# A two-stage gated layer on one core: first-stage tiles only centred, their roots applied a step later in silu and gate

## The reference

```
def _layernorm(x, axis=-1, eps=1e-05):
    m = jnp.mean(x, axis=axis, keepdims=True)
    v = jnp.var(x, axis=axis, keepdims=True)
    return (x - m) / jnp.sqrt(v + eps)
...
        for e in range(E):                      # E = 4, each 512 x 512, Wg = Wu = Wd = ctx[e]
            g = jax.nn.silu(jnp.einsum('bsd,fd->bsf', hidden_states, Wg[e]))
            u = jnp.einsum('bsd,fd->bsf', hidden_states, Wu[e])
            y = jnp.einsum('bsf,df->bsd', g * u, Wd[e])
            out = jnp.where((expert_ids == e)[..., None], y, out)
...
    x = x + jnp.tanh(g_xattn[0]) * _L0_xattn_ref(_layernorm(x, axis=-1), itok_BxS_13_99985, ctx_2048, ctx_2048, ctx_2048)
    x = x + jnp.tanh(g_ffn[0]) * _L0_ffn_ref(_layernorm(x, axis=-1), ...)   # shared MLP + top 2 of 16 experts
```

## Time and profile before

| | |
|---|---|
| median of 3 runs | 477.52 us (477.21 to 477.65) |
| the profiled execution's own time | 477.07 us |
| its span, first to last instruction | 474.9 us |
| granted TensorE clock, mean | 0.997 |
| PE busy | 459.0 us (97% of the span) |
| DVE, ACT, POOL busy | 329.8, 254.8, 209.0 us |

### The profile page before, as it was taken

One profiled execution on the slowest core, in us unless ns is written; L12 is line 12 of the kernel. 1 busy time (PEld: TensorE's weight loads), 2 busy tenths in 40 slices (PEclk: granted clock), 3 DMA queues, 4 the chain that ended last, 5 costly groups with the idle time before them and its releaser, 6 DMA issues.

```text
span 474.9 us, 7818 instructions
## 1 busy us (share of the span) xinstructions
PE 459.0 (97%) x2493; PEld 392.5 (83%) x2493; DVE 329.8 (69%) x726; ACT 254.8 (54%) x379; POOL 209.0 (44%) x176
## 2 busy tenths in 40 slices
PE   2899999999999999999999999999999999999995
PEld 1477878888888888888888999999999999999994
DVE  6689999998986844488649776766666666676442
ACT  5664445545553443542436566566556766656441
POOL 0513444555442475435177343434425444342543
PEclk9999999999999999999999999999999999999998
DMA  8643666886664542363379988898868988888364
GB/s 302 196 167 126 195 198 210 277 258 236 214 212 162 179 122 112 85 82 46 44 192 203 286 287 265 274 285 262 254 206 251 270 256 268 258 277 243 47 129 91
DMA packets 30476, 95.28 MB, mean 201 GB/s; under 512 B 4976, under 2 KB 7024, under 8 KB 29936
## 3 DMA queue, kind: packets, MB, share of 16 engines
q0 software_dynamic: 17056, 43.92, 37.7%
q1 hardware_dynamic: 13104, 50.98, 31.3%
q10 hardware_dynamic: 288, 0.01, 0.0%
HBM read 67.77 MB, written 28.70 MB: 203 GB/s over the span
## 4 chain that ended last, share of the span: by engine, by line
PE 92%; DVE 4%; DMA 1%; issue 1%; ACT 0%; POOL 0%; POOLq 0%; DVEq 0%
PE psG L1370 50%; PE psY L1370 30%; PE psT L1375 8%; PE psG L1626 1%; DMA front<-in_x,idx 1%; DMA tok_i<-in_ids 1%; PE psY L1387 1%; PE psG L1399 1%; DVE stats L991 0%; PE psY L1506 0%; POOL out L560 0%; PE psY L1670 0%; DVE xh_sb L964 0%; DVE gu L980 0%; PE psY L1532 0%
## 5 line engine op out<-in xcount | busy, mean ns | idle before, releaser
L1370 PE MATMUL psY<-arena 128*128 (+1 forms) x366 | 89.2, 394 | 0.0
L1370 PEld LDWEIGHTS psY<-arena 128*128 128x128 f32 x366 | 67.7, 188 | 13.9
L519 POOL DMA_INDIRECT ht<-out,idx x32 | 32.6, 1018 | 68.3 <-PE psT L1375 52.5
L1370 PE MATMUL psY<-slot,arena 128*128 128x512 f32 x240 | 59.0, 394 | 0.0
L1114 DVE TENSOR_TENSOR slot<-raw,slot 128x1536 fp32r<-128x1536 f32 x25 | 43.8, 1757 | 21.0 <-ACT slot L660 21.0
L1370 PE MATMUL psG<-arena 128*128 x228 | 57.0, 399 | 0.0
L1114 DVE TENSOR_TENSOR arena<-raw,arena 128x1536 fp32r<-128x1536 f32 x24 | 42.0, 1757 | 17.5 <-ACT arena L660 17.4
L1370 PEld LDWEIGHTS psY<-slot,arena 128*128 128x128 f32 x240 | 44.3, 188 | 9.2 <-ACT xh_sb L704 0.2
L1370 PE MATMUL psG<-arena,slot 128*128 128x512 f32 x216 | 51.3, 392 | 0.0
L1370 PEld LDWEIGHTS psG<-arena 128*128 128x128 f32 x228 | 41.5, 188 | 8.5 <-issue 0.4
L1370 PEld LDWEIGHTS psG<-arena,slot 128*128 128x128 f32 x216 | 40.1, 188 | 8.2
(11 more groups left out here) (246 smaller groups left out, 811.3 us busy)
## 6 DMA issues: line engine op xcount, KB each, us to landing
raw<-in_w SPq DMA_DIRECT2D x48, 768.0 KB, 5.5
padded<-xh_sb SPq DMA_DIRECT2D x19, 256.0 KB, 2.2
raw<-in_w SPq DMA_DIRECT2D x12, 192.0 KB, 4.3
raw<-in_ctx_t SPq DMA_DIRECT2D x2, 1024.0 KB, 8.1
ht<-in_ctx_t SPq DMA_DIRECT2D x1, 1024.0 KB, 11.1
xh_sb<-in_ctx_t SPq DMA_DIRECT2D x1, 1024.0 KB, 9.1
out<-log_sb SPq DMA_DIRECT2D x4, 256.0 KB, 7.9
ht<-out,idx POOLq DMA_INDIRECT x33, 4.2
```

The costliest lines, as they stand in the source:

```text
L519: pool.indirect_dma_start(ht[:, n, :], None, halves_of_out, slots(e * NA + a, 0)).then_inc(g_here[n], 16)
L1370: ins = pe.matmul(ps, left[a], right[b], start=n == 0 and m == 0, stop=n == total - 1 and m == 2)
```

## The change

It makes h of a tile without its root. `centre` writes mean minus x (ACT; for tile 0 a DVE instruction), and the reciprocal root of the row is applied to G: as the scale of silu, and as the scalar of the gate product (`root_of(t)`). The minus sign is met by negated context parts (`high_ctx` with scale -1, `low_ctx` as `raw*-1 - high`, `rest` with the matrix `minus`) and a negated tanh of the first gate. The roots of tiles 0 to 2 come from one chain of three columns in step -1 (`root3`); that of tile t+1 comes in step t, in one chain with that of the residual rows.

For the residual rows, the second `bn_stats` is gone. The residual instruction also gives its row sum (`accum_out`), a small instruction makes the negated mean, and ACT sums the squares of the centred rows (`ACT.Square` with a bias and `accum_out`). The chain's head waits for them (`sq_done`). ACT's step has a new order: high part of g, squares of tile t-2, centring of tile t+2, silu, high part of h, normalised residual rows.

In the opening, part 1 is now half on DVE, ahead of the first statistics and behind POOL's first two gathers (`first_out`), half by PE and ACT; part 2 is wholly on DVE in steps 0 and 1; `high_ctx(2)` moves behind `take_rest(1, 2)`. PE no longer does `rest(2, i)`, and waits for one `take_rest` rather than four. G(0) is issued as three groups of four matmuls, each behind its own operand. POOL's gather 1 goes ahead of its memset. The four DMAs of zeros move into SP's loop, one each behind `padded` of tiles 9 to 12.

```diff
+        mv = sb("mv", [P, 4, 2])
+        root = sb("root", [P, 4, 2])
+        root3 = sb("root3", [P, 3])
+        x1_sum, x1_mean, x1_sq, shift = (sb(n, [P, 4]) for n in ("x1_sum", "x1_mean", "x1_sq", "shift"))
...
+        def root_of(t):
+
+            return root3[:, t:t + 1] if t < 3 else root[:, (t - 1) % 4, 0:1]
...
-            sp.wait_ge(zeroed, 1)
-            for a, b in ((a, b) for a in range(NA) for b in range(2)):
-                sp.dma_start(out[TOK + a * P:TOK + (a + 1) * P, b * D:(b + 1) * D], zeros[:, :]).then_inc(spare_sent, 16)
...
+                elif 9 <= t <= 12:
+                    if t == 9:
+                        sp.wait_ge(zeroed, 1)
+                    a, b = divmod(t - 9, 2)
+                    sp.dma_start(out[TOK + a * P:TOK + (a + 1) * P, b * D:(b + 1) * D], zeros[:, :]).then_inc(spare_sent, 16)
...
             gather_xa(0)
+            gather_xa(1)
             pool.memset(cur[:, :], 0).then_inc(first_out, 1)
-            for t in range(1, 4):
+            for t in range(2, 4):
...
+            act.activation(tg[:, 0:1], gate_in[:, 0:1], ACT.Tanh, scale=-1.0).then_inc(tg_ready, 1)
+            act.activation(tg[:, 1:2], gate_in[:, 1:2], ACT.Tanh).then_inc(tg_ready, 1)
...
-                act.activation(ctx_hi[:, e * KD * D:(e + 1) * KD * D], ctx_raw(e), ACT.Copy).then_inc(ctx_hi_done, 1)
+                act.activation(ctx_hi[:, e * KD * D:(e + 1) * KD * D], ctx_raw(e), ACT.Copy,
+                               scale=-1.0).then_inc(ctx_hi_done, 1)
...
+                act.wait_ge(rest_ps, e * (KD - 2) + i + 1)
-                    act.wait_ge(ctx_lo_done, 2)
+                    act.wait_ge(ctx1_half, 1)
...
-            high_ctx(2)
...
+            def centre(t, src):
+
+                act.wait_ge(mv_done, t + 1)
+                if t >= 2:
+                    act.wait_ge(hT_ps, t - 1)
+                act.activation(h[:, t % 2, :], src, ACT.Identity, scale=-1.0, bias=mv[:, t % 4, 0:1]).then_inc(h_ready, 1)
...
+                if have(known, -2):
+
+                    act.wait_ge(mean_ready, t - 1)
+                    act.activation(xh_sb[:, par, D:2 * D], xh_sb[:, par, 0:D], ACT.Square,
+                                   bias=x1_mean[:, (t - 2) % 4:(t - 2) % 4 + 1],
+                                   accum_out=x1_sq[:, (t - 2) % 4:(t - 2) % 4 + 1]).then_inc(sq_done, 1)
+                if have(known, 2) and known >= 2:
+                    centre(t + 2, xa_of(t, par, known))
...
+                    act.wait_ge(root_ready, max(t - 1, 1))
+                    act.activation(s_sb[:, 0:D], psG[0][:, :], ACT.Silu, scale=root_of(t)).then_inc(s_ready, 1)
...
-                    take_rest(2, 1)
-                    take_rest(2, 2)
+                    centre(1, xa[:, 1, :])
+                    take_rest(1, 2)
+                    high_ctx(2)
                 if known == 0:
-                    take_rest(2, 3)
-                act.wait_ge(norm_ready, t + 3)
...
+                    take_rest(1, 3)
+                    centre(2, xa_of(0, 0, 0))
+                if known == 1:
+                    centre(3, xa_of(1, 1, 1))
                 if have(known, -2):
-                    norm(xh_sb[:, par, D:2 * D], xh_sb[:, par, 0:D], 1, xh_ready)
+                    act.wait_ge(norm_ready, t - 1)
+                    act.activation(xh_sb[:, par, D:2 * D], xh_sb[:, par, 0:D], ACT.Identity,
+                                   scale=root[:, t % 4, 1:2], bias=shift[:, t % 4:t % 4 + 1]).then_inc(xh_ready, 1)
...
+                return dve.scalar_tensor_tensor(ctx_lo[:, c], ctx_raw(e)[:, part * n:(part + 1) * n], -1.0,
+                                                as_f32(ctx_hi[:, c]), ALU.mult, ALU.subtract)
...
+            dve.wait_ge(first_out, 1)
+            low_ctx(1, 0, 2).then_inc(ctx1_half, 1)
+            dve.wait_ge(tg_ready, 2)
...
+            def newton_root(first, out, cols):
+
+                V, Y, T = (nwt[:, m, cols] for m in range(3))
+                each = range(cols.start, cols.stop)
+
+                def weighed():
+                    return [dve.scalar_tensor_tensor(nwt[:, 2, c:c + 1], nwt[:, 0, c:c + 1], nwt[:, 1, c:c + 1],
+                                                     nwt[:, 1, c:c + 1], ALU.mult, ALU.mult) for c in each]
+
+                nw(*first)
+                nw(dve.tensor_scalar(Y.bitcast(I32), V.bitcast(I32), -0.5, float(RS_MAGIC - (1 << 31)),
+                                     ALU.mult, ALU.add))
+                nw(*weighed())
+                nw(dve.scalar_tensor_tensor(Y, T, -((27 / 4 * RS_W) ** (1 / 3)), Y, ALU.add, ALU.mult))
+                nw(*weighed())
+                nw(dve.scalar_tensor_tensor(T, T, -10 / 3 * RS_W, T, ALU.add, ALU.mult))
+                return dve.scalar_tensor_tensor(out, T, 5 * RS_W ** 2, Y, ALU.add, ALU.mult)
...
+                def residual():
                     dve.wait_ge(y_ps, t - 1)
                     dve.wait_ge(xb_here[par], landed(t - 2, par))
...
                     dve.scalar_tensor_tensor(xh_sb[:, par, 0:D], psY[0][:, :], tg[:, 0:1], xb[:, par, :],
-                                             ALU.mult, ALU.add).then_inc(x1_ready, 1)
+                                             ALU.mult, ALU.add, accum_out=x1_sum[:, c:c + 1]).then_inc(x1_ready, 1)
+
+                def residual_mean():
+                    c = (t - 2) % 4
+                    dve.wait_ge(x1_ready, t - 1)
+                    dve.tensor_scalar(x1_mean[:, c:c + 1], x1_sum[:, c:c + 1], -1.0 / D, None,
+                                      ALU.mult).then_inc(mean_ready, 1)
...
-                    dve.tensor_tensor(gu[:, 0:D], s_sb[:, 0:D], psG[0][:, :], ALU.mult).then_inc(gu_ready, 1)
+                    dve.scalar_tensor_tensor(gu[:, 0:D], psG[0][:, :], root_of(t), s_sb[:, 0:D],
+                                             ALU.mult, ALU.mult).then_inc(gu_ready, 1)
+
+                if known == FIRST:
+                    dve.wait_ge(xa_here[0], 16)
+                    bn(0, xa[:, 0, :])
+                    mean(0)
+                    dve.wait_ge(mv_done, 1)
+                    dve.tensor_scalar(h[:, 0, :], xa[:, 0, :], mv[:, 0, 0:1], -1.0,
+                                      ALU.subtract, ALU.mult).then_inc(h_ready, 1)
+                    dve.wait_ge(xa_here[1], 16)
+                    bn(1, xa[:, 1, :])
+                    mean(1)
+                elif known == FIRST + 1:
+                    low_h()
+                    xa_landed(dve, 0, 0, 0)
+                    bn(2, xa_of(0, 0, 0))
+                    mean(2)
+                    dve.wait_ge(mv_done, 3)
+                    newton_root([variance(0, slice(0, 3))], root3[:, :], slice(0, 3)).then_inc(root_ready, 1)
+                elif known == 0:
                     gate1()
                     low_h()
+                    link(low_ctx(2, 0, 2))
+                elif known == 1:
+                    low_g()
+                    dve.wait_ge(ctx_lo_done, 2)
+                    low_ctx(2, 1, 2).then_inc(ctx_lo_done, 1)
+                    gate1()
+                    low_h()
...
+                    bn(t + 2, xa_of(t, par, known))
+                    mean(t + 2)
+                else:
+                    if known == 2:
+                        low_g()
+                    residual()
                     if one:
...
+                        bn(t + 2, xa_of(t, par, known))
+                    residual_mean()
+                    if one:
+                        mean(t + 2)
+                    if known > 2:
+                        low_g()
+                    if known == NT + 1:
...
                     if known == 2:
                         dve.wait_ge(ctx_lo_done, 3)
                         low_ctx(3, 1, 2).then_inc(ctx_lo_done, 1)
-
+                        gate1()
+                        low_h()
...
+                    more = have(known, 1)
+                    if more:
+                    dve.wait_ge(sq_done, t - 1)
+                    square = dve.tensor_scalar(nwt[:, 0, 1:2], x1_sq[:, c:c + 1], RS_C / D, EPS * RS_C, ALU.mult, ALU.add)
+                    if more:
+                        i = newton_root([square, variance(t + 1, slice(0, 1))], root[:, t % 4, :], slice(0, 2))
                     else:
+                        i = newton_root([square], root[:, t % 4, 1:2], slice(1, 2))
+                    i.then_inc(root_ready, 1)
+                    dve.wait_ge(root_ready, t)
+                    dve.tensor_tensor(shift[:, t % 4:t % 4 + 1], x1_mean[:, c:c + 1], root[:, t % 4, 1:2],
+                                      ALU.mult).then_inc(norm_ready, 1)
+                    if have(known, 0) and known > 2:
+                        gate1()
+                    if have(known, 1) and known > 2:
+                        low_h()
+                if known == 1:
+                    link(low_ctx(3, 0, 2))
...
+                pe.matmul(psG[i][:, :], as_f32(minus[:, :]), ctx_raw(e)[:, s], start=True, stop=False)
...
-            rest(2, 0)
```

(16 more changed lines are left out.)

115 lines of the change are left out of this document (27 added, 88 removed).

## The result

The changed kernel takes **473.62 us** (median of 6 runs, 473.35 to 474.17), against 477.58 (476.91 to 477.87) for the kernel before on the same chip: a ratio of 0.992, 95% interval 0.9909 to 0.993. The forecast was 473.9. Its profiled execution took 473.53 us with a span of 471.6 (before 477.07 and 474.9), at the same granted clock, so the span is 3.3 us shorter. This compares one profile with one; by the medians the gain is 3.96 us.

A forecast was written before the change was run, and what follows sets the result against it. PE, busy 97% of the span, was taken to bound the kernel. Gains of 2.8 and 2.05 less 0.96 and 0.3 took the profile's 477.07 to 473.5; the median stands 0.45 above, so 473.9 us (own range 472.8 to 475.0; full range 472.2 to 476.0).

The forecast's parts named there:

- G(0) at 19.5: Opening: with h ready at 17.6 and PE's rest(1,2) ending at 19.5, the first product starts 3.85 us sooner.
- G(1) at 25.3, bound by take_rest(1,3): Step 1: G(1) waits for part 1, whose take_rest ends at 24.45, then 0.4 restart and 0.44 transposes; 2.9 us gain left.
- The looser bound: Step 1: silu and gate of tile 0, with the three-column root done at 22.4, would allow G(1) at 24.85.
- Part 3 free till 26.3, landing at 25 to 26 "without the zeros": Opening: part 3's 1 MB lands at 25 to 26; its high copy ahead of silu(1) on ACT is free till 26.3.
- rival (1): Opening: part 3 lands late, at 28.0, so G(3) slips by 1.7 us and the time is 475.6; chance 0.14.
- (c): Step 2: silu(2) starts at 36.15 behind ACT's squares and centring; gT(2) waits 0.46, G(3) at 38.95, 2.8 us sooner.
- (d): Step 2: the root chain and residual(1) make low_g(2) 0.96 us late in front of Y(2); G(4) at 46.3.
- The steady step: Steps from 4: after Y(t-2) ends at T, mean T + 1.75, squares T + 2.75, chain T + 4.6, low_h T + 5.95; 0.6 spare.
- The rival of a bounding handshake: Stage 1's mean, squares and chain bound each step: beyond 0.6 us extra, each 0.1 costs 0.1 in 16 steps; 479.5, chance 0.07.
- Tables: ACT: rival that Square needs another activation table than silu, two 1.28 us loads a step in 17 steps, 511; chance 0.02.
- Nothing behind stage 1 takes the gain back: Behind stage 1: PE is busy there throughout, so the gain of stage 1 stays.
- the sum: Whole kernel: 2.8 us at G(3) plus 2.05 old stalls less 0.96 new stall, 3.9, with 0.3 taken off.

The follow-up runs named there:

- run 6: The changed kernel with two more passes of Square on ACT in every middle step, ahead of the real one: 492.15 us, ratio 1.032.
- run 8: The changed kernel with part 3's DMA behind tile 1's rows and, in step 20, the last residual's squares behind both row copies: 472.85 us, ratio 0.9909.
- Run 3: The changed kernel with the context parts in the old order (part 1 on DVE, part 2 by PE and ACT): 476.6 us, ratio 0.9971.
- run 7: The changed kernel with DVE's half of part 1 moved from ahead of the first statistics to behind h(0): 473.58 us, ratio 0.993.
- Run 1: The changed kernel with the four DMAs of zeros back in the opening, behind part 3 in SP's queue: 474.33 us, ratio 0.9923.
- run 2: The changed kernel with part 3's DMA issued when gather 1 has landed, not gather 2: 473.97 us, ratio 0.9921.
- Run 10: The changed kernel with silu(2) ahead of ACT's squares, low_g(2) ahead of residual(1), tile 0's normalised rows behind g(2)'s high part: 474.12 us, ratio 0.9927.
- run 5: The changed kernel with one more pass of Square on ACT in every middle step, ahead of the real one: 479.18 us, ratio 1.0043.
- runs 2 to 6: Five runs; the one without its own line put the residual's statistics back on DVE (`bn_stats`, no squares) in the changed kernel: 474.87 us, ratio 0.9942.
- runs 9 and 10: The first of the two: the changed kernel with tile 0's root worked out by itself, ahead of the low part of h(0): 474.3 us, ratio 0.9938.

## Why the prediction came out as it did

The time was right, 473.62 for 473.9, and by the mechanism that I gave: an earlier opening, part of it lost in steps 0 to 3, and the old stalls recovered. That it came within 0.3 us is partly luck, as the sum at the end of this section shows. Its steps, one by one:

- **G(0) at 19.5:** 19.60. The multiply of 512 float32 took 0.48 for 0.45. The path was another one: I had h and its transposes as the last to come, but PE was still busy with the rests of part 0 until 18.07, when h had been done for 0.4 us. Where those rests ran fast sooner, G(0) came at 19.13 (run 6); where later, at 20.41 (run 8). I called PE's work before G(0) small and gave these rests no term. Run 3 shows that the order of the parts carries this start: h was done as early there, and G(0) came at 22.33.
- **G(1) at 25.3, bound by take_rest(1,3):** 25.31 in the timeline, and the wait is for that copy. It ended at 24.76 for 24.45, and the restart to G took 0.55 where I had 0.84: two errors that met. The looser bound was nearly as tight: the root was done at 23.0, not 22.4, and ACT came to the copy at 24.16 when its rest was done at 24.04.
- **Part 3 free till 26.3, landing at 25 to 26 "without the zeros": this step failed.** It landed at 27.05, 7.5 us after an issue that was itself 0.6 late (19.52 for 18.92, run 7). Run 1 shows no part of the zeros in it. The cost was small, silu(1) at 28.91 and 0.32 us at G(4) (run 2), as the landing came 1 us sooner than in rival (1). What sped it up from the 9.1 us of before is open.
- **(c):** gate(2) ended at 38.02; by the working of (c) it is 38.08. But G(3) came at 39.15 in the timeline, not 38.95. The sum for it (31.7, 2.75, 0.44, 2.73, the wait of 0.46, and 0.87 of transposes) leaves out the restart that the text names; from the gate's end to G(3) are 1.13 us in the trace. And the order on ACT alone does not make the wait. With the same order and part 3 in time (run 2) no wait stands at gT(2), and from G(2) to G(3) are 6.95 us instead of 7.40.
- **(d):** Y(2) waited 0.63 for low_g(2), and with the restart G(3) to G(4) took 7.49 us in the timeline, 1.14 over the plain 6.35, where I had 0.96. Run 10 removes this wait and meets another of 1.14 at gT(4), so no single order causes the loss.
- **The steady step:** mean, squares and chain end came at T + 1.5, T + 2.3 and T + 4.5, for 1.75, 2.75 and 4.6; low_h ended at T + 5.74 for 5.95. The predicted slack of 0.6 doesn't follow from its own times: it is T + 6.55 less T + 5.95, but PE's next Y ends at T + 6.35, which leaves 0.4. That DVE was then idle for 0.65 is luck, made by a round that was 0.2 shorter. The slack measured by loading it is 0.83. I had the accumulator reads at 0.06 and 0.2: 0.08 and 0.19. The Trainium skill (VectorE: DVE Perf Modes, Two Vector instructions with no wait between them) counts such a Vector instruction as two. The trace agrees, with a row of its own for DVE's read. It spoke against the change by 0.08 us a step, within the slack. The rival of a bounding handshake needed one more pass of 0.76 to come true (run 5), but its price was far too low. By its rule (nothing up to 0.6, then 0.1 for each 0.1 in 16 steps) such a pass costs 2.6 us; it cost 5.9, as steps 2 to 7 and those with split_chunks had almost no slack.
- **Tables:** no table load shows in stage 1; Square runs beside silu, identity and copy. The Trainium skill (ScalarE: Activation LUTs, Table sets: the hidden batching unit) does not name it among the functions in every set; the trace settles it for these. The rival's price of 511 put its 34 us on the time before; put on the forecast it is 508.
- **"Nothing behind stage 1 takes the gain back":** nearly so. 3.33 us at G(12) were 3.17 at 172.20: the squares stand ahead of the copies of transposed rows on ACT, and PE waits 0.15 us for one of their low parts (run 8 wins this back). What I missed is the last rows' path through `padded`: in five profiles (runs 2 to 6) its gather took 1.2 to 1.4 us longer to land than in the changed kernel's, and PE waited for it, 0.40 us in run 2.

Of the sum, 2.8 plus 2.05 less 0.96 less 0.3, the first term was mis-sized and measured 2.34. Of the missing 0.46, 0.2 is the later start of G(3). The other 0.25 was never there: 38.95 is built from durations, as starts in the timeline are, and was taken from the chain's 41.74, where the timeline has 41.49 for the same product. The stalls net of the new one gave 0.99 by G(12) for 1.09. The 0.3 taken off made up for part of that, and 3.3 us of span came out for 3.6 forecast. The forecast of 473.5 for the profile's own time was met (473.53) only because 0.24 us less lay outside the span than before; and the median stands 0.09 above that time, not 0.45. None of these tenths is sharp, since like openings differ by up to 1.3 us between profiles.

## What to carry to other kernels

An earlier operand is worth only as much as the queues ahead of its consumer allow: h was ready 2.3 us sooner, and the order of the context parts decided whether PE could take it. When a wait goes, look for the next one at almost the same time: two edits here (runs 9 and 10) each removed a visible wait and met the next behind it. A single profile of a small edit can mislead: run 2 gained 0.32 us in the middle and lost it to a DMA that landed 1.2 us later, as it also did in runs without that edit. Starts are compared within one kind of view, timeline or chain. Slack in a handshake is best measured by loading it with a known extra, twice, since the difference of the two gives the price and the first gives the room.

## What the runs showed of the hardware

- A pass over 128x512 with an accumulator is followed by a read instruction of its own: 0.08 us on DVE, 0.19 on ACT, here without a stall.
- POOL's issue of an indirect DMA took 1.90 us beside a DVE instruction with two SBUF inputs, and 0.95 when that was moved (run 7). In four places of the openings such an issue began while a DVE instruction over 512 columns or more ran from SBUF to SBUF, and each ended 0.81 to 0.82 us behind that instruction's end: 1.90 us at 15.16 and 1.09 at 17.36 in the changed kernel (the latter beside the 0.48 us multiply), 1.25 at 18.77 in run 7, and 1.62 at 24.95 in the kernel before. An issue that was under way when DVE began, and one beside statistics (20.02 in the changed kernel), took 0.95.
- Part 3, 1 MB from memory, took 6.3 to 8.7 us to land in the profiles of the changed kernel and the runs (9.1 before); with 1 MB of stores behind it in the same queue it took 7.6 (run 1). The gather of the last rows took 3.3 us in the changed kernel and 4.5 in run 2, though the path up to its issue is equally long; over all runs it took 3.2 to 3.6 or 4.5 to 4.7.
- In the opening, the same fp32r matmul took 1.41 us and later 0.80, with the granted clock at 1.00 of full speed throughout. The switch came between about 14 us (run 6) and 17 us (run 8), and most of the spread of G(0), from 19.13 to 20.41 us, goes with it. The runs don't show why.
